# Cross-attention with a quantized feed-forward: attended values split in SBUF and transposed by DMA, three steps moved to ScalarE, new order

## The reference

```python
# x [32,100,256], ctx [32,361,256], mask [1,1,100,361], WQ WK WV [16,256,64], WO [1024,256]
xn = layernorm(x)
Q, K, V = einsum(xn, WQ), einsum(ctx, WK), einsum(ctx, WV)        # per head
logits = Q @ K.T / sqrt(64) + mask * -1e9
A = softmax(logits) @ V                                           # [b, h, t, 64]
x = x + concat_heads(A) @ WO
y = layernorm(x)
x = x + qlinear(gelu(qlinear(y, W1, b1)), W2, b2)                 # 256 -> 1024 -> 256
# qlinear: activations to 8 bits with one scale and zero point from the min and max over
# the WHOLE tensor, weights to 8 bits with one symmetric scale
```

## Time and profile before

| | |
|---|---|
| median of 3 runs | 1209.32 us (1203.5 to 1209.76) |
| the profiled execution | 1213.14 us |
| its span | 1211.3 us |
| PE busy | 1069.4 us (88%) |
| DVE busy | 1047.3 us (86%) |
| ACT busy | 785.4 us (65%) |
| POOL busy | 672.1 us (55%) |
| mean granted PE clock | 0.962 |

### The profile page before, as it was taken

How to read it: one execution, slowest core, us unless ns; L and a number is a source line. 1 busy time by engine, 2 the same in 40 slices (tenths; PEclk the granted TensorE clock), 3 DMA queues, 4 the chain that set the end, 5 groups by cost and what they waited for, 6 DMA issues and landing times.

```text
span 1211.3 us, 38088 instructions
## 1 busy us (share of the span) xinstructions
PE 1069.4 (88%) x10801; PEld 688.4 (57%) x10801; DVE 1047.3 (86%) x2827; ACT 785.4 (65%) x1553; POOL 672.1 (55%) x934
## 2 busy tenths in 40 slices
PE   4997889999999999999999999999999999985719
PEld 2553556666666666656656665666566656654318
DVE  5775789999999999989989998999899989984996
ACT  4654666666666666666666666666666666663915
POOL 2332556666666666666666666666666666653000
PEclk9998999999999999999999999999999999995959
DMA  8201555555555555555545554555455545550003
GB/s 260 73 1 35 102 96 107 107 107 107 107 107 107 107 107 107 107 105 106 106 97 107 107 107 94 107 107 107 101 107 107 107 101 107 107 113 18 1 0 109
DMA packets 383299, 117.01 MB, mean 97 GB/s; under 512 B 361956, under 2 KB 382252, under 8 KB 383276
## 3 DMA queue, kind: packets, MB, share of 16 engines
q1 hardware_dynamic: 383276, 116.72, 45.6%
HBM read 25.29 MB, written 3.28 MB: 24 GB/s over the span
## 4 chain that ended last, share of the span: by engine, by line
PE 42%; DVE 23%; issue 15%; DMA 8%; POOL 5%; ACT 4%; DVEq 2%; SPq 1%; POOLq 0%; ACTq 0%
PE front L334 10%; PE front L335 9%; PE front L336 9%; DMA pT<-hl 7%; PE back L1173 4%; POOL hl L553 4%; DVE hl L891 4%; DVE prob L878 3%; DVE k_l L903 2%; DVE hrange L1015 2%; DVE hrange L1016 2%; PE tp L1155 2%; PE front L1155 2%; ACT v L667 2%; PE front L1244 1%
## 5 line engine op out<-in xcount | busy, mean ns | idle before, releaser
L553 POOL TENSOR_TENSOR hl<-prob,hl 100x361 f16<-100x361 f32 x512 | 433.7, 864 | 331.5 <-ACT hl L659 230.6
L652 ACT ACTIVATE prob<-prob,nmax 100x361 f32<-100x361 f32 x512 | 294.7, 588 | 5.7 <-DVE nmax L878 3.2
L663 ACT ACTIVATE k_h<-front 128x362 f16<-128x362 f32 x256 | 120.8, 472 | 196.4 <-PE front L336 190.6
L1173 PEld LDWEIGHTS back<-v,pT 128*128 128x128 f16 (+1 forms) x4608 | 180.1, 98 | 79.9 <-DMA pT<-hl 30.3
L1173 PE MATMUL back<-v,pT 128*128 128x65 f16 (+1 forms) x4608 | 194.9, 194 | 29.0 <-DMA pT<-hl 24.9
L667 ACT ACTIVATE v<-front 128x512 f16<-128x512 f32 (+1 forms) x192 | 114.8, 598 | 108.1 <-PE front L336 94.6
L334 PE MATMUL front<-ctx_h,wk_h 128*128 128x362 f16 x512 | 167.7, 328 | 6.1 <-DVE v L909 2.5
L336 PE MATMUL front<-ctx_h,wk_l 128*128 128x362 f16 x512 | 165.3, 323 | 0.0
L335 PE MATMUL front<-ctx_l,wk_h 128*128 128x362 f16 x512 | 165.2, 323 | 0.0
L903 DVE SCALAR_TENSOR_TENSOR k_l<-front,k_h 128x362 f16<-128x362 f32 x256 | 132.9, 527 | 34.0 <-ACT k_h L663 34.0
L334 PE MATMUL front<-wv_h,ctx_h 128*128 128x512 f16 (+1 forms) x384 | 147.8, 385 | 6.4 <-DVE k_l L903 6.4
(11 more groups left out here) (180 smaller groups left out, 2023.0 us busy)
## 6 DMA issues: line engine op xcount, KB each, us to landing
ctx_raw<-ctxT SPq DMA_DIRECT2D x33, 361.0 KB, 3.3
pT<-hl SPq DMA_TRANSPOSE x512, 2.6
xs<-x SPq DMA_DIRECT2D x8, 400.0 KB
q_all<-x SPq DMA_DIRECT2D x32, 100.0 KB
out<-xb SPq DMA_DIRECT2D x32, 100.0 KB
q_all<-wq SPq DMA_DIRECT2D x1, 1024.0 KB, 6.3
q_all<-wk SPq DMA_DIRECT2D x1, 1024.0 KB, 12.3
q_all<-wv SPq DMA_DIRECT2D x1, 1024.0 KB, 14.4
```

Of the source, the lines that this page charges most:

```text
L553: pool.tensor_tensor(hl[0:T, n % RP, 1, 0:S], prob[0:T, n % RP, 0:S], hl[0:T, n % RP, 0, 0:S], ALU.subtract).then_inc(s_lo, 1)
L652: act.activation(prob[0:T, n % RP, 0:S], prob[0:T, n % RP, 0:S], ACT.Exp, bias=nmax[0:T, n:n + 1], scale=-1.0).then_inc(s_exp, 1)
L1173: ins = pe.matmul(obank[j % 2][:, n % GH * DV:(n % GH + 1) * DV], pT[0:r, n % RP, part_ * ST + st, :], v2[half][0:r, st, v, n % HT, :], st ...
```

## The change

Six things change, in one step.

1. The transposes of `att` leave PE. `att` and its high half become [100, 256] tiles for four heads with two slots. AH (new, ACT) copies the high half to `ahl`, AL (new, POOL) writes the low half, AD (new, SP) issues a DMA transpose of both, `attT<-ahl`, four times per batch. The steps AT on PE, ACT and DVE go. WO waits for two of these transposes. The shared PSUM banks have 16 users per batch where they had 18.
2. y of the layer norm is one ACTIVATE with scale and bias (YN, ACT). POOL adds epsilon and makes the bias, two instructions more beside the power. DVE has five LN steps where it had seven.
3. MG moves from DVE to ACT.
4. The high half of 11 of 16 heads is copied on ACT (before 8) and of heads 2, 5, 8, 11, 14 on DVE.
5. One more memset (`ahl`) at the start of the second stage; ScalarE also waits there for the scaled mask.
6. All order tables are new.

```diff
+VH = (2, 5, 8, 11, 14)
+AH = tuple(h for h in range(H) if h not in VH)
...
 SP_STEPS = at(
-    DT=(6.663, 7.216, 7.432, 8.255, 8.436, 9.654, 10.624, 11.493, 17.158, 18.147, 18.435, 18.707, 18.784,
-        20.491, 21.193, 21.559),
+    DT=(1.935, 1.994, 2.541, 2.865, 4.257, 6.643, 7.179, 7.775, 8.441, 13.428, 14.435, 15.378, 15.933, 16.455,
+        16.934, 17.469),
+    AD=(15.172, 15.797, 18.188, 18.441),
...
-    att = place("att", [P, HD], F32)
-    attT_h = place("attT_h", [P, NM, T], F16)
-    attT_l = place("attT_l", [P, NM, T], F16)
+    att = place("att", [P, 2, GH * DK], F32)
+    ahl = place("ahl", [P, 2, 2, GH * DK], F16)
+    attT = place("attT", [P, NG, 4, TR], F16)
...
+                elif kind == "AD":
+                    wait_alone(sp, s_al, NG * a + n + 1)
+                    wait_alone(sp, s_wp, 2 * a + n // 2 - 1)
+                    sp.dma_start_transpose(attT[:, n, :, :], ahl[0:TR, n % 2, :, :]).then_inc(s_ad[n], 16)
...
+                elif kind == "AL":
+                    wait_alone(pool, s_ah, NG * a + n + 1)
+                    pool.tensor_tensor(ahl[0:T, n % 2, 1, :], att[0:T, n % 2, :], ahl[0:T, n % 2, 0, :],
+                                       ALU.subtract).then_inc(s_al, 1)
                 elif kind == "RSTD":
-                    wait_alone(pool, s_ln, LN_STEPS * a + 3)
+                    wait_alone(pool, s_ln, LN_STEPS * a + 2)
+                    pool.tensor_scalar(row[0:T, 8:9], row[0:T, 7:8], EPS, None, ALU.add).then_inc(s_rl, 1)
+                    wait_alone(pool, s_rl, 3 * a + 1)
                     pool.tensor_tensor(row[0:T, 9:10], row[0:T, 8:9], mhalf[0:T, 0:1], ALU.pow).then_inc(s_rl, 1)
+                    wait_alone(pool, s_rl, 3 * a + 2)
+                    pool.tensor_scalar(row[0:T, 8:9], row[0:T, 6:7], row[0:T, 9:10], -1.0, ALU.mult,
+                                       ALU.mult).then_inc(s_rl, 1)
...
-                elif kind == "AT":
-                    wait(act, s_ap, 2 * a + n + 1)
-                    wait(act, s_wp, 2 * a + n - 1)
-                    act.activation(attT_h[:, 4 * n:4 * n + 4, :], ps[:, 0:4 * T].rearrange("p (m t) -> p m t", m=4),
-                                   ACT.Copy).then_inc(s_ah, 1)
+                elif kind == "AH":
+                    wait(act, s_nrm, NG * a + n + 1)
+                    if n < 2:
+                        wait(act, s_wp, 2 * a)
+                    else:
+                        act.wait_ge(s_ad[n - 2], 16 * (a + 1))
+                    act.activation(ahl[0:T, n % 2, 0, :], att[0:T, n % 2, :], ACT.Copy).then_inc(s_ah, 1)
+                elif kind == "YN":
+                    wait(act, s_rl, 3 * a + 3)
+                    act.activation(yn_slot(a), x1_slot(a), ACT.Identity, scale=row[0:T, 9:10],
+                                   bias=row[0:T, 8:9]).then_inc(s_yn, 1)
+                elif kind == "MG":
+                    wait(act, s_max, H * a)
+                    wait(act, s_sv, 4 * a + 4)
+                    act.activation(mask_g[0:T, 0:S], mask_b[0:T, 0:S], ACT.Identity, scale=gain[0:T, 1:2]).then_inc(s_mg, 1)
+                    act.activation(ngain[:, :], gain[:, 0:1], ACT.Copy, scale=-1.0).then_inc(s_mg, 1)
...
-                    wait(pe, s_nrm, NG * a + NG // 2 * (n + 1))
-                    for i in range(4):
-                        ins = pe.transpose(ps[:, i * T:(i + 1) * T], att[0:T, (4 * n + i) * P:(4 * n + i + 1) * P],
-                                           ident[0:T, 0:T])
-                    ins.then_inc(s_ap, 1)
                 elif kind == "WO":
-                    wait(pe, s_at, 2 * a + n + 1)
+                    pe.wait_ge(s_ad[2 * n], 16 * (a + 1))
+                    pe.wait_ge(s_ad[2 * n + 1], 16 * (a + 1))
```

More of the change, by code:

```diff
@@ L60 @@
 CREDIT = 16
-LN_STEPS = 7
+LN_STEPS = 5
 RP = 4
@@ L112 @@
-SP_STEPS = at(
-    DT=(6.663, 7.216, 7.432, 8.255, 8.436, 9.654, 10.624, 11.493, 17.158, 18.147, 18.435, 18.707, 18.784,
-        20.491, 21.193, 21.559),
-    CTX=(-10.816,),
-    X=(15.657,))
-POOL_STEPS = at(
[L118 to L126, removed]
+    K=(-3.272, -3.218, 0.417, 3.177, 5.402, 5.589, 6.88, 8.009),
@@ new lines @@
+    V=(-0.389, -0.158, 3.93, 4.476, 5.715, 6.941),
+    QP=(0.323, 0.324, 5.089, 5.09, 6.385, 6.386, 11.073, 11.074),
+    PV=(5.493, 5.494, 6.882, 7.431, 8.326, 10.092, 11.373, 12.161, 14.542, 17.812, 19.125, 19.346, 19.721,
+        20.537, 20.842, 21.088),
+    WO=(19.656, 22.766),
+    CT=(-10.913,))
+ACT_STEPS = at(
+    K=(-3.034, -1.421, 0.677, 1.229, 3.873, 4.974, 7.515, 9.882),
+    V=(0.056, 0.343, 3.08, 3.262, 5.01, 8.922),
+    EXP=(1.241, 2.455, 2.846, 3.247, 4.119, 4.903, 5.173, 5.763, 7.295, 7.904, 10.398, 12.108, 12.5, 15.943,
+        16.16, 16.715),
+    HA=(2.705, 2.895, 3.632, 4.707, 5.839, 7.246, 8.236, 12.788, 15.939, 16.208, 16.879),
+    AH=(12.892, 13.17, 18.329, 19.525),
+    YN=(25.514,),
+    MG=(0.582,),
+    C=(-5.776, -5.59),
+    Q=(-4.378, 3.111))
@@ new lines @@
+DVE_STEPS = at(
+    K=(-5.772, -5.215, -1.83, -0.54, 4.917, 5.603, 7.395, 8.556),
+    V=(-3.751, -2.607, 3.892, 4.536, 5.797, 8.093),
+    WO=(18.128, 22.816),
+    MAX=(-2.223, -1.219, 0.106, 2.345, 4.411, 4.791, 5.136, 5.186, 6.162, 6.888, 7.859, 8.468, 8.818, 10.36,
+        11.239, 11.281),
+    HV=(3.021, 5.371, 7.538, 10.048, 13.34),
+    NORM=(9.41, 9.722, 15.223, 19.921),
+    CMAX=(-13.64,),
+    CRED=(-11.59,),
+    SCALE=(-10.214,),
+    LN=(23.14, 23.242, 24.6, 25.24, 25.891))
+SP_STEPS = at(
+    DT=(1.935, 1.994, 2.541, 2.865, 4.257, 6.643, 7.179, 7.775, 8.441, 13.428, 14.435, 15.378, 15.933, 16.455,
+        16.934, 17.469),
+    AD=(15.172, 15.797, 18.188, 18.441),
+    CTX=(-20.152,),
+    X=(16.092,))
@@ L129, in turn @@
+POOL_STEPS = at(
+    LO=(0.57, 1.131, 1.67, 2.824, 3.805, 3.837, 5.331, 8.094, 9.396, 12.032, 12.425, 13.172, 14.375, 15.104,
+        15.265, 15.859),
+    AL=(12.894, 13.68, 16.537, 18.129),
+    C=(-5.321, -4.607),
+    Q=(-2.816, 1.382),
+    RSTD=(25.284,),
+    CS=(-10.913,),
+    M=(16.37,),
+    XB=(25.962,))
+JOBS = {step: t for step, t in PE_STEPS.items() if step[0] in ("K", "V", "WO")}
 def turn(events, part, in_first={}):
@@ L314, in build @@
     s_ri, s_nrm = sem("s_ri"), sem("s_nrm")
-    s_ap, s_ah, s_at = sem("s_ap"), sem("s_ah"), sem("s_at")
+    s_ah, s_al = sem("s_ah"), sem("s_al")
+    s_ad = [sem(f"s_ad{n}") for n in range(NG)]
     s_wp, s_x1 = sem("s_wp"), sem("s_x1")
@@ L641, in _ @@
             q_chunk(c, c % 2)
-        start(act, (s_kh, s_vh, s_ah, s_exp, s_ha, s_ch, s_qh))
+        start(act, (s_kh, s_vh, s_ah, s_exp, s_ha, s_yn, s_ch, s_qh))
         def act_turn(b, part, steps=slice(None)):
@@ L693, in _ @@
         phase1_over(act)
-        wait(act, s_zero, 8)
+        wait(act, s_zero, 9)
+        act.wait_ge(s_mb, 1)
         act_turn(-1, "first", LATER)
@@ L848, in _ @@
         low_w(0, 0)
-        start(dve, (s_k, s_v, s_cm, s_cr, s_sv, s_at, s_max, s_mg, s_hv, s_ri, s_nrm, s_x1, s_ln))
+        start(dve, (s_k, s_v, s_cm, s_cr, s_sv, s_max, s_mg, s_hv, s_ri, s_nrm, s_x1, s_ln))
         x_low(0, 0)
@@ L861, in _ @@
         dve.tensor_scalar(mask_b[0:T, 0:S], mask_b[0:T, 0:S], -1.0e9, None, ALU.mult).then_inc(s_mb, 1)
-        wait(dve, s_zero, 8)
+        wait(dve, s_zero, 9)
         dve.wait_ge(s_mb, 1)
@@ L921, in dve_turn @@
                     ctx_unit(a)
-                elif kind == "AT":
-                    wait(dve, s_ah, 2 * a + n + 1)
-                    dve.tensor_tensor(attT_l[:, 4 * n:4 * n + 4, :], ps[:, 0:4 * T].rearrange("p (m t) -> p m t", m=4),
-                                      attT_h[:, 4 * n:4 * n + 4, :], ALU.subtract).then_inc(s_at, 1)
                 elif kind == "WO":
@@ L1051, in _ @@
     def _(pe):
-        start(pe, (s_kp, s_vp, s_ap, s_wp, s_qk, s_pv, s_ct))
+        start(pe, (s_kp, s_vp, s_wp, s_qk, s_pv, s_ct))
         pe.wait_ge(s_id, 2)
@@ L1117, in bank_read @@
             else:
-                wait(pe, s_at if kind == "AT" else s_x1, 2 * a + n + 1)
+                wait(pe, s_x1, 2 * a + n + 1)
         def pe_turn(b, part):
```

65 lines of the change are left out of this document (15 added, 50 removed).

## The result

| | before | after |
|---|---|---|
| median | 1209.34 us (1203.5 to 1209.76) | 1279.14 us (1278.31 to 1280.69, 4 runs) |
| profiled execution (span) | 1213.14 us (1211.3) | 1280.69 us (1278.9) |
| ratio | | 1.0579 [1.0537, 1.0621] |

What follows compares the result with a forecast made beforehand. It took SP's queue and a loop of waits through it as the bound, a 31.0 us turn: 1213.1 + 21.7 - 8 + 3 = 1230 us, 1226 on the median's scale, range 1196 to 1250.

Steps and rivals of the forecast that it cites:

- Four AD: New transposes on SP's queue: 0.86 us hold plus 0.26 between, 1.12 each, 4.48 us per turn.
- in proportion to the blocks: Lower estimate of an AD's hold on SP: four of six blocks of a 1.20 us transpose, 0.80 us.
- a fixed part like that of a plain DMA: Upper estimate of an AD's hold on SP: 0.32 + 4/6 x 0.88 = 0.91 us.
- an AD costs as much as a DT: Rival on SP: an AD holds 1.20 us, loop 32.4 us, 1269 us on the median's scale; chance 0.12.
- The loop: Waits through SP, ACT and POOL from head 9's transpose to the next turn's: 31.0 us, taken as the new turn.
- the twelve others and X: On SP between DT9 and DT5+: twelve transposes of 1.46 us and X at 0.96 us.
- landing until ScalarE starts the copy of head 9: From the start of head 5's transpose, DT5+, to its landing, which ACT's copy awaits: 2.6 us.
- ScalarE to the context's second copy: On ACT, head 9's copy, V5, YN, K7, C0 and EXP, up to C1: 2.85 us.
- from there to DT9: C1 on ACT, through POOL's low halves and LO9, to SP's transpose: 1.49 + 0.83 + 0.28 = 2.60 us.
- SP was the full engine: SP's own turn grows from 25.83 to 30.31 us without any wait, so savings on DVE and PE cannot show.
- The dips: Clock drops to 1.2 GHz in before's loop: about 8 of 1.6 us, 13.0 us; 8 us counted back.
- Head and tail: Kernel's start and end: a 0.9 us memset, and 2 us more for the last part; together 3 us.

Runs made afterwards that it cites:

- ha6_late: The changed kernel with ScalarE's copy of head 9 moved from the end of a turn to behind the context's second copy in the next; 1264.73 us, 1.0468.
- no_ad: The changed kernel without its four new DMA transposes; the output projection multiplies fixed weights instead of the attended values; 1162.78 us, 0.9613.
- before_plus4: The kernel before with four extra two-block DMA transposes per turn on SP, from fixed weights into a tile nobody reads; 1296.28 us, 1.0716.
- dt_pair: The kernel before with one DMA transpose of twelve blocks per two heads instead of one per head; 1326.21 us, 1.0976.
- dt_pair_after: The changed kernel, its four AD kept, with one DMA transpose per two heads for the probabilities; 1350.96 us, 1.1181.

## Why the prediction was wrong

**The step that failed** is the term "Four AD", where I wrote "I take 0.86, between these two", and 1.12 with what lies between. Measured, an AD holds SP for 1.184 us, and the four slots from an AD to the next transpose are 1.58, 1.51, 1.43 and 1.49: 6.01 us where I had 4.48. Of these 1.53 us, 1.30 are the hold and the rest is the spacing. I chose between "in proportion to the blocks" and "a fixed part like that of a plain DMA". Both were models; my one row, sixteen transposes of one width, told nothing of how the hold depends on width. The case that an AD costs as much as a DT was among my rivals, with the right mechanism and 1269 us, and I gave it 0.12, though it was the only end of the range that was a row for a transpose at all. The plain DMA's 0.32 to 0.41 is a row of another kind of instruction, and I let it pull the value down.

The rule of the Trainium skill that I weighed ("DMA: Bandwidth & Descriptors", the section on why a DMA increments its semaphore by 16) has one push per tile for a transpose from SBUF to SBUF. I read it as a hold in proportion to the blocks, which grows by a sixth of 1.20, 0.20 us, per block. The runs show 0.0095 us per block from two to eight, beside a fixed 1.146 us. That proportion does not describe the hold of this instruction on SP here, and the fixed part decides.

**The loop, term by term**, from the transpose at 595.62 to that at 628.33:

| | predicted | measured |
|---|---|---|
| DT9 to DT5+: four AD slots | 4.48 | 6.01 |
| the twelve others and X | 18.48 | 18.88 |
| landing until ScalarE starts the copy of head 9 | 2.60 | 2.68 |
| ScalarE to the context's second copy | 2.85 | 2.61 |
| from there to DT9 | 2.60 | 2.53 |
| turn | 31.0 | 32.71 |

Of the 1.7 us that were missing, 1.53 are the AD. Another 0.40 are on SP in the slots of the others: 0.30 of it in the three gaps between a DT and the AD behind it, 0.31 to 0.38 us and not the 0.26 of the earlier trace rows, where the order shows more register and semaphore instructions. The parts on ScalarE and POOL are 0.31 shorter than I had them, the landing 0.08 longer.

**What held.** SP was the full engine, and the loop through head 9's copy closed nearly as described, but into CTX and not into DT9; ha6_late confirms it and shows what it is worth: 0.5 us of 2.4. With the loop opened, SP waits 0.3 us and the turn is still 32.2: the rest is the queue. The sums of the others were near: DVE 24.6 (24), ACT 23.7 (24.8), POOL 23.0 (23.3), but PE 28.6 where I had 27.3. It has the eight instructions fewer that I counted (305 against 313), and rows of the same shape are as long as before (194 ns against 193 for PV, 320 against 319 for a projection of keys). no_ad has the same matmuls in 27.87 us. Busy time counts rows that overlap once; what makes it longer here was not pursued. An AH takes 0.41 us and an AL 0.69, inside their bounds. PE waits at WO for an AD for 0.7 us in the turn, and 27.0 in all, against the 116 us that no_ad gained.

**The dips.** Of the 13.0 us that before's loop has above 31 turns of 30.30, 8.0 lie in five turns of 31.9 with one dip each, and 5.0 in the first two turns, which have two more (clock 0.95 over 65.6 us). So there are seven, not "about 8", and if the first two cost 1.6 each as the others do, some 2 us of the 13.0 are no dips at all. The changed kernel has one, in its first two turns (0.97), which are 2.2 above two of 32.7. I counted 8 of the 13 us back. That the five dips of the later turns cost just this is luck, since I had thought that they would still occur and be taken up by PE's slack. In the changed kernel they do not occur, and a less busy PE does not explain that, as the last section shows. What I had in mind can be seen in before_plus4, which keeps its dips: a turn with one and the turn behind it, 66.78 us, are only 0.2 longer than two of the 33.28 that a turn without takes.

```profile
649.28:683.16 33.88, 30.43 (x309) 18.84 (x309) 28.07 (x82) 21.06 (x45) 19.77 (x27) 0.95 0.50 103
683.16:716.06 32.90, 28.96 (x309) 18.29 (x309) 28.02 (x84) 21.18 (x45) 19.76 (x27) 1.00 0.50 103
```

**Head and tail** cost 5.0 us (3). Together with 31 x 1.74 = 53.9 us for the turns and 13.0 in place of 8 for what was above ordinary turns, the misses sum to 53.9 - 5 + 2 = 50.9, against the 50.7 us from 1230 to 1280.7.

## What to carry to other kernels

Before moving transposes from the tensor engine to DMA, lay the instructions of the queue that issues them in order of time: it has no busy row, and here it was already 26 us full in a turn of 30. In this kernel a DMA transpose of two to eight blocks costs a nearly fixed 1.2 us there, plus 0.25 to 0.4 between two. So where the data can wait, issue fewer and wider ones. Where it goes round a small ring of slots, that lost here. When a cost has no row of its own, start from the nearest row of the same kind of instruction; a proportion is a guess, to be priced as such.

## What the runs showed of the hardware

- A DMA transpose of f16 blocks of 112 rows holds SP's queue for 1.165, 1.184, 1.203 and 1.222 us at 2, 4, 6 and 8 blocks; at 12 blocks it is 1.26 to 1.36 (the same row in dt_pair, below). The time to landing grows more with the width: 2.3, 2.4, 2.6, 2.9 and 3.5 us.

```profile
L468 SPq DMA_TRANSPOSE pT<-hl x256: 1260/1359/1462, 116.8 to 1206.9; - x128
DMA to landing us min/median/max: 3.4/3.5/5.1
```

- A dip of the clock cost 1.6 us in before, where PE is busy for 28.5 us of a turn of 30.3, and 0.2 in before_plus4, where it is 29.0 of 33.3.
- Whether the clock dips in the loop did not follow from a full PE. From 130 to 1000 us, the row of no_ad, with PE busy for 96%, and then that of dt_pair_after, 82%:

```profile
130.00:1000.00 870.00, 830.95 (x9013) 530.18 (x9011) 748.00 (x2152) 708.17 (x1557) 682.16 (x956) 1.00 0.54 111
```

```profile
130.00:1000.00 870.00, 711.33 (x7466) 437.94 (x7462) 608.22 (x1780) 596.16 (x1292) 567.87 (x792) 0.96 0.53 105
```

  The kernels built on the one before, at 84 to 94%, are all at 0.99; those built on the changed one are at 1.00, but for the two with paired heads at 0.96. So it is not PE's transposes of `att` either, which those two lack. What decides it stays open.
